# Hex convolution with four PSUM banks a chunk: one opening matmul a chunk, and two matmul streams that run through the whole chunk

## The reference

```python
xp = jnp.pad(x, ((0, 0), (0, 0), (1, 1), (1, 1)))
xp = xp.at[:, :, DST_R, DST_C].set(xp[:, :, SRC_R, SRC_C])
up = _conv(xp, w_up * jnp.asarray(_UP), b_up)
left = _conv(xp, w_left * jnp.asarray(_LEFT), b_left)
right = _conv(xp, w_right * jnp.asarray(_RIGHT), b_right)
out = out.at[:, :, 0::2, 0::2].set(up)
out = out.at[:, :, 1::2, 0::2].set(left)
out = out.at[:, :, 1::2, 1::2].set(right)
return out * jnp.asarray(OUT_MASK)
# and: x = x + conv(_gn(x))
```

## Time and profile before

| what | value |
|---|---|
| median of 3 runs | 754.72 us |
| the profiled execution's own time | 756.86 us |
| its span in the profile | 755.1 us |
| PE busy | 704.7 us, 93% |
| DVE busy | 676.3 us, 90% |
| ACT busy | 576.4 us, 76% |
| POOL busy | 489.1 us, 65% |
| data moved by DMA | 269.23 MB |

### The profile page before, as it was taken

How to read it: one execution, slowest core, us unless ns; L and a number is a source line. 1 busy time by engine, 2 the same in 40 slices (tenths; PEclk the granted TensorE clock), 3 DMA queues, 4 the chain that set the end, 5 groups by cost and what they waited for, 6 DMA issues and landing times.

```text
span 755.1 us, 36563 instructions
## 1 busy us (share of the span) xinstructions
PE 704.7 (93%) x15762; PEld 635.4 (84%) x15762; DVE 676.3 (90%) x1793; ACT 576.4 (76%) x1258; POOL 489.1 (65%) x1115
## 2 busy tenths in 40 slices
PE   0999999999999999999999999999999999999974
PEld 0888999899899989998988888898888888888864
DVE  5899999999999999989989999999999999999900
ACT  2687787778777877788787787787787787787853
POOL 1177667766776677667567567667667667667663
PEclk9999999999999999999999999999999999999996
DMA  9999999999999999999999999999999999999983
GB/s 261 328 360 378 377 382 377 368 359 369 364 367 380 366 364 365 364 357 369 363 361 370 369 375 371 366 377 366 375 372 364 378 369 372 362 379 372 357 288 121
DMA packets 265022, 269.68 MB, mean 357 GB/s; under 512 B 2640, under 2 KB 264784, under 8 KB 264976
## 3 DMA queue, kind: packets, MB, share of 16 engines
q1 hardware_dynamic: 264976, 269.23, 104.4%
HBM read 135.01 MB, written 134.22 MB: 357 GB/s over the span
## 4 chain that ended last, share of the span: by engine, by line
DMA 51%; PE 40%; ACT 2%; issue 2%; DVE 2%; POOL 1%; SPq 1%; POOLq 0%; ACTq 0%
PE bank L449 38%; DMA xs<-in_x 29%; DMA out<-xs 20%; DMA xs<-in_L_conv_w_right 2%; POOL xs L393 1%; ACT res L338 1%; DVE stats L222 1%; PE bank L428 1%; PE bank L461 1%; ACT tn L309 1%; SPq L173 0%; ACT xs L351 0%; SPq L177 0%; DVE m L235 0%; POOL tn L404 0%
## 5 line engine op out<-in xcount | busy, mean ns | idle before, releaser
L449 PE MATMUL bank<-tn,wts 64*64 64x192 f32 (+5 forms) x15600 | 690.3, 323 | 8.0 <-issue 8.0
L449 PEld LDWEIGHTS bank<-tn,wts 64*64 64x64 f32 x15600 | 616.1, 137 | 42.7 <-issue 8.1
L393 POOL TENSOR_TENSOR xs<-res,xs 128x192 f32<-128x192 f32 (+6 forms) x780 | 389.7, 537 | 80.1 <-ACT res L338 80.0
L222 DVE BATCH_NORM_STATS2 stats<-xs 128x6 f32<-128x512 f32 x512 | 346.9, 690 | 39.3 <-DMA xs<-in_x 39.3
L338 ACT ACTIVATE res<-bank,bias 64x512 f32<-64x512 f32 (+6 forms) x650 | 304.1, 468 | 73.1 <-PE bank L449 64.0
L309 ACT ACTIVATE tn<-xs,nmr,rstd 128x256 f32<-128x256 f32 x511 | 258.9, 592 | 5.4 <-DVE nmr L265 3.8
L404 POOL COPY tn<-tn 128x128 f32<-128x128 f32 (+2 forms) x320 | 97.9, 361 | 180.3 <-ACT tn L309 180.3
L270 DVE TENSOR_SCALAR tn<-xs,rstd,nmr 128x256 f32<-128x256 f32 x513 | 207.4, 474 | 2.3
L303 ACT ACTIVATE std<-var 128x16 f32<-128x16 f32 x64 | 13.4, 210 | 90.2 <-DVE var L243 90.2
L461 PEld LDWEIGHTS bank<-blank 128*128 128x128 f16 x130 | 12.5, 96 | 49.1 <-issue 42.0
L461 PE MATMUL bank<-blank 128*128 128x2 f16 x130 | 23.0, 177 | 15.3 <-POOL tn L404 14.4
(11 more groups left out here) (18 smaller groups left out, 35.8 us busy)
## 6 DMA issues: line engine op xcount, KB each, us to landing
xs<-in_x SPq DMA_DIRECT2D x63, 2048.0 KB, 16.9
out<-xs SPq DMA_DIRECT2D x63, 2048.0 KB, 17.1
xs<-in_x SPq DMA_DIRECT2D x4, 512.0 KB, 5.7
out<-xs SPq DMA_DIRECT2D x2, 1024.0 KB, 5.3
xs<-in_L_conv_w_up SPq DMA_DIRECT2D x1, 256.0 KB, 8.3
xs<-in_L_conv_w_left SPq DMA_DIRECT2D x1, 256.0 KB, 9.0
xs<-in_L_conv_w_right SPq DMA_DIRECT2D x1, 256.0 KB, 11.3
bias<-in_L_conv_b_up SPq DMA_DIRECT2D x2, 0.2 KB, 7.5
```

What stands on the lines that cost most here:

```text
L222: last = nc.vector.bn_stats(stats[:, k % 2, 2 * u:2 * u + 2].rearrange("p g a -> p (g a)"), both)
L393: last = nc.gpsimd.tensor_tensor(onto, view(res, at, [(rows * w, pairs), (w, rows), (1, w)]), onto, ALU.add)
L449: last = nc.tensor.matmul(psum[bank + j][to:to + C, at:at + cols], wts[first:first + C, NT * rect[0] + n, :], taps(b, rect, tap, g0, pairs ...
```

## The change

`convolve` has one wait and one gate a chunk instead of two. The matmuls of banks 0 and 2 make one stream and those of banks 1 and 3 another; the rule that takes the next tap from the stream with fewer columns issued runs over the whole chunk. Matmuls, weights, banks and what the other engines do stay as they are.

```diff
+from itertools import chain
 CROSSED = (False, True, False, True)
+STREAMS = ((0, 2), (1, 3))
@@ bank_taps
                     at += cols
-                yield 0
@@ convolve
                 bank = NB * (b if bank is None else bank)
-                for js in ((0, 1), (2, 3)):
-                    pe.wait_ge(bank_empty, NB * k + js[1] + 1)
-                    gate(bank + js[0])
-                    work = [bank_taps(b, bank, j, g0, pairs) for j in js]
-                    spent = [0, 0]
-                    cols = [next(w) for w in work]
-                    while any(cols):
-                        n = min((m for m in range(2) if cols[m]), key=lambda m: spent[m])
-                        spent[n] += cols[n]
-                        cols[n] = next(work[n])
+                pe.wait_ge(bank_empty, NB * (k + 1))
+                gate(bank)
+                work = [chain.from_iterable(bank_taps(b, bank, j, g0, pairs) for j in js)
+                        for js in STREAMS]
+                spent = [0, 0]
+                cols = [next(w) for w in work]
+                while any(cols):
+                    n = min((m for m in range(2) if cols[m]), key=lambda m: spent[m])
+                    spent[n] += cols[n]
+                    cols[n] = next(work[n], 0)
```

## The result

The changed kernel takes 753.1 us (median of 15 runs, 750.73 to 754.44) against 755.75 us for the kernel before (15 runs, 754.32 to 757.86). The ratio over all the runs is 0.9954 (the two medians alone give 0.9965), with a 95% interval of 0.994 to 0.9967: faster by 0.46%, just inside the half per cent that was called hardly to be told from none. The profiled execution's span is 751.4 us against 755.1.

A forecast was written before the change was run, and what follows sets the result against it. The DMA rate was taken to bound the kernel from about 126 to 701 us, covering PE's saving. Median 754.72 - 0.4 (DMA stage) - 1.3 (tail) = 753.0 us; range 747.5 to 758.5.

The forecast's parts named there:

- The reading by PE's busy share: Whole kernel: PE is the bound after all and the time falls with it, to 720 us; chance 0.03.
- the seam: PE's chunk, around the second gate: 0.36 us, of which about 0.15 is the last matmul still streaming; 0.2 net saved.
- the imbalance: PE's chunk: a pair lasts as long as its longer stream; two streams take 4480 columns instead of 4640, saving 0.35 us.
- that rival: PE's chunk: the two streams hold each other up and the change does nothing for PE; 754.7 us, chance 0.14.
- The DMA stage: From about 126 us to the last load's landing near 701: sum taken as -0.4 us, ends +1.1 and -1.5.
- The loss from an earlier blocked queue: SP's queue blocks near 95 us instead of 126 to 131: 35 us at 3% less DMA rate, +1.1 us.
- The earlier stage of just-in-time loads: Lead of the loads used up near 215 us, then 370 instead of 366 GB/s: 135 us x 1.1%, -1.5 us.
- The third case: From 215 us on: an idler PE leaves the DMA more, perhaps 375 GB/s, -6 us, so 747; chance 0.16.
- The tail: Behind the loop, chunks 62, 63a and 63b: sum -1.3 us, ends nothing and -3.
- the second stall: PE's "issue" wait of 4.19 us in 63a: follows store 62, which moves 0.55 earlier, so -0.55 us.
- 63b: Half-width last piece of chunk 63: two savings of 0.2 and 0.17 in PE's work, -0.35 us.
- The other side: DMA to the end: a longer backlog in the queue means 366 GB/s instead of 370, +5.2, so 759.7; chance 0.10.

The follow-up runs named there:

- the transfers alone: Loads and stores in SP's order of before, with no weights and no computing, each store waiting for its own load: 716.81 us, ratio 0.9465 to the kernel before.
- seven gates: The changed kernel with seven gates in a row at the head of each chunk instead of one: 755.99 us, ratio 0.9976 to the kernel before.
- Two taps of five: The changed kernel with only the first and last tap of each rectangle, three of five left out: 731.81 us, ratio 0.9676 to the kernel before.
- the old loop: The changed kernel with the pairs and two gates of before in the loop, new code in chunks 62, 63a and 63b: 755.98 us, ratio 0.9982 to before.
- the new loop with the old tail: The changed kernel with the pairs and two gates of before in chunks 62, 63a and 63b only: 752.5 us, ratio 0.9931 to the kernel before.

## Why the prediction was right, and where its terms were off

**The bound.** This was right, and is shown: the DMA covers PE. Taking a quarter of the bytes away turned less than 4 us into 44, and the transfers alone take 717. The reading by PE's busy share (720 us, chance 0.03) is out.

**PE's chunk.** 10.2 was forecast, 10.09 measured; the saving is 0.69 instead of 0.55, near the upper bound of 0.71. Both terms were too small where they are taken one after the other: the seam was put at 0.2 and costs 0.27 between pairs, the imbalance at 0.35 and is worth 0.42 once the gate is gone. (Taken the other way round they are 0.52 and 0.17.) For the 0.15 us that were subtracted as "the last matmul still streaming" no row was given, and no run shows them. The streams do not hold each other up, so that rival fell.

**The DMA stage.** This is the term that was mis-sized. The queue was blocked from about 99 us against 95, and the waits for wraps began near 225 against 215. The term was -0.4 with ends of +1.1 and -1.5, and 3.5 us is what the middle lost: outside its ends. Three things stand behind it in the windows. The loss from an earlier blocked queue did not appear: from 95 to 130 us the rate is 377 GB/s in the changed kernel, with its queue blocked, against 379 before. The earlier stage of just-in-time loads came as forecast and a little larger, 372 against 367 GB/s from 215 to 350, first before, then changed:

```profile
215.00:350.00 135.00, 135.00 (x3035) 122.15 (x3031) 130.91 (x345) 110.20 (x239) 93.24 (x211) 1.00 1.07 367
215.00:350.00 135.00, 122.06 (x2896) 112.16 (x2892) 126.07 (x334) 106.73 (x228) 89.92 (x201) 1.00 1.07 372
```

And that stage itself became quicker, 372 against 370 from 350 to 690, which the sum held fixed. Each of the last two is worth about 1.8 us (1.3% of 135, 0.5% of 340). The third case expected such a rise, to 375 and worth 6 us, from an idler PE. But with seven gates PE is nearly as idle and most of the gain is gone, so idle time by itself is not what the runs show. Over the whole stretch from 130 to 690 the rate rose from 369 to 371 GB/s, less than the 1% that was to show the prediction wrong; from 130 to 350 alone it rose by 1.1%.

What in PE's work the DMA feels is not settled. Two taps of five and the transfers alone show that from 130 us on PE's work slows the DMA. Seven gates show that a pace within 0.2 us of the changed kernel's is not enough for the gain. That the 128 x 128 gates, beyond their share in time, are what costs the DMA would fit all rows, but no kernel without gates was tried, and six more gates cost about as much as the one second gate did, which a simple price per gate doesn't give.

**The tail.** The forecast was -1.3, as -0.55 from the second stall, -0.35 in 63b, -0.42 from the last stall. Measured from the landing to the end it is -1.5 and -1.8 in the two profiles of the changed kernel against the one of before, but -2.2 behind the old loop and only -0.1 to -0.4 behind the new one. So the size is not confirmed, and the way was partly wrong. The third stall went, as forecast. The first swallowed PE's gain, as forecast. The second did too, against the forecast: its end stands 7.03 us behind the end of the first before and after, and 36.17 us behind the last landing in both (737.33 - 701.16, 735.11 - 698.94), though the store of chunk 62 was issued 0.56 sooner counted from that landing:

```profile
726.80 0.37 SPq L175 DMA_DIRECT2D out<-xs  x1
```

So the block of code doesn't come behind that store. The distance from edge to edge is 7.03 us in five of the six profiles with code behind the loop; in the sixth, the new loop with the old tail, it is 732.94 - 726.19 = 6.75:

```profile
726.19 3.59 PE L451 MATMUL bank<-tn,wts 64*64 64x96 f32 x128 [1.77 <-issue]
732.94 0.90 PE L451 MATMUL bank<-tn,wts 64*64 64x64 f32 x12 [3.16 <-issue]
```

What sets it stays open. Between the two profiles of before and after, all of the tail's gain lies in 63b: from the second stall's end to PE's end it took 9.33 us before (746.66 - 737.33) and 7.88 after (742.99 - 735.11). But the old tail took 8.19 there behind the new loop, where its last stall is absent too. Part of the size is PE's granted clock, a mixture of its two levels: 0.67 before and 0.65 after in this stretch, which makes any saving larger.

**The other side.** In this rival a blocked queue was to cost DMA rate to the end. It did not: 370 and 372 GB/s where a mean below 367 was to decide for it.

The predicted 753.0 for a measured 753.1 owes something to luck. It was built on a median of 754.72 from three runs, where 15 gave 755.75: 1.03 too low. The medians differ by 2.65 where the sum had 1.7: 0.95 too little. The two errors cancel. The profiles differ by more, and there the DMA term alone is short by 3.1 us; the first store, 1.4 us later in the changed kernel's profile, hides a part of that. The half clock in 63b is no reason to take the profiled run as an outlier: all six profiles of full kernels with a halved last chunk have it there (a granted clock of 0.65 to 0.76).

## What to carry to other kernels

When an engine is busy for 93% of the time, ask how long its finished work waits before it is used: 11 us between the last addition and the store said that PE could lose 40 us of work and the time would hardly move. To prove such a cover, cut what is thought to cover (here a quarter of the bytes) and run both versions. Code written out behind a loop has to be fetched while everything waits; look for "issue" stalls a fixed number of instructions apart at the end of a program, since removing them was worth more here than the whole change.

## What the runs showed of the hardware that I had not expected

- The DMA's rate, with its engines full all the time, depends on what PE does, but only from about 130 us on: 380 and 381 GB/s with no computing, 377 to 379 with two fifths of the matmuls, 366 to 372 with all. From 60 to 130 us it is 377 to 379 in all three.
- A gate behind a gate is cheap (six more cost 0.15 us), a gate among 64 x 64 matmuls is dear (0.27 to 0.52 us). That it is the change between the two shapes that costs fits both, but no gate of 64 x 64 was tried.
- A block of 128 matmuls with their weight loads took 7.03 us from edge to edge behind the loop in five profiles and 6.75 in a sixth, while PE had 2.5 us of work in it in the changed kernel (7.03 - 4.49). The Trainium skill's "mostly hidden" ("Runtime: NRT & Kernel Launch", Instruction fetch mechanics) doesn't hold here: the two stalls are 7.2 us in the changed kernel, and without code behind the loop its time falls by about 0.9% (0.9848 against 0.9937, beside each other).
